# A new order for the steps between the last local-attention tile and the first softmax of the second layer

## The reference

```python
x = x + _L0_attn_ref(_layernorm(x), A, BC)        # a linear recurrence over the tokens
x = x + _L0_ffn_ref(_layernorm(x), ...)           # 2 layers of local attention (8 heads, windows of 64) with a gelu MLP
x = x + _L1_attn_ref(_layernorm(x), Wq, ...)      # full softmax attention, 8 heads of 16 columns
x = x + _L1_ffn_ref(_layernorm(x), ...)           # a shared expert and one of 32 routed experts per token
```

```python
xn = (x - mu) * rsqrt(var + LN_EPS) * gamma + beta
q = xn @ Wq + bq ; k = xn @ Wk + bk ; v = xn @ Wv + bv
scores = q @ k.T / sqrt(dk)                        # per batch and head, 512 x 512
p = softmax(scores) ; att = p @ v
out = att.reshape(S, B, D, H).sum(axis=-1)
```

## Time and profile before

| | us |
|---|---|
| median of three runs | 655.63 |
| the profiled execution, whole | 654.95 |
| its span from first to last instruction | 653.1 |
| PE busy | 594.9 (91%) |
| DVE busy | 515.4 (79%) |
| ACT busy | 364.2 (56%) |
| POOL busy | 308.8 (47%) |

### The profile page before, as it was taken

The page is one execution under the profiler, slowest core; times in us unless marked ns, Lnnn a source line. Parts: engine busy times, 40 slices in busy tenths (PEclk is TensorE's granted clock), DMA queues, the critical chain, the costliest instruction groups (busy, mean ns, idle before and its releaser), DMA issues.

```text
span 653.1 us, 14782 instructions
## 1 busy us (share of the span) xinstructions
PE 594.9 (91%) x5571; PEld 362.7 (56%) x5571; DVE 515.4 (79%) x919; ACT 364.2 (56%) x582; POOL 308.8 (47%) x254
## 2 busy tenths in 40 slices
PE   8777987999999999999999889888999989998994
PEld 7455665766766676667667566543232324454442
DVE  5887888889889798898898966877778776575883
ACT  0233453477566575674775563413765577634882
POOL 4664464556455646464665742513210010261886
PEclk8998999999999999999999999998999999998998
DMA  8413010010010101010101144151975336215441
GB/s 257 105 33 107 18 35 9 18 33 10 21 32 18 27 17 27 17 26 19 34 10 28 24 112 99 45 105 54 241 183 159 109 96 219 67 36 127 62 48 11
DMA packets 33298, 44.04 MB, mean 67 GB/s; under 512 B 9248, under 2 KB 24652, under 8 KB 32460
## 3 DMA queue, kind: packets, MB, share of 16 engines
q1 hardware_dynamic: 26172, 40.97, 23.9%
q0 software_dynamic: 3968, 2.12, 2.5%
q10 hardware_dynamic: 3088, 0.01, 0.3%
HBM read 27.54 MB, written 8.41 MB: 55 GB/s over the span
## 4 chain that ended last, share of the span: by engine, by line
PE 64%; DVE 15%; ACT 7%; issue 7%; POOL 4%; DMA 1%; POOLq 0%; DVEq 0%; SPq 0%; ACTq 0%
PE ps L1652 6%; PE ps L1683 4%; PE ps L1605 4%; PE ps L1553 3%; PE ps L1890 3%; PE ps L1661 3%; PE ps L1538 3%; PE ps L1580 3%; PE ps L1624 3%; PE ps L1788 3%; PE ps L1539 3%; PE ps L1613 3%; PE ps L1590 3%; PE ps L1544 3%; PE ps L1772 3%
## 5 line engine op out<-in xcount | busy, mean ns | idle before, releaser
L693 POOL TENSOR_TENSOR rnorm<-ssum_c,neg_half 128x16 f32<-128x16 f32 x32 | 94.7, 2960 | 102.1 <-DVE ssum_c L1099 100.7
L1328 DVE TENSOR_REDUCE mneg<-ps 128x2 f32<-128x1024 f32 x64 | 77.5, 1220 | 20.8 <-PE ps L1772 19.8
L701 POOL TENSOR_TENSOR region_r<-region_b,region_w 128x512 f32<-128x512 f32 x60 | 77.7, 1316 | 33.9 <-DVE region_b L1104 33.0
L929 ACT ACTIVATE region_r<-ps 128x1024 f32<-128x1024 f32 x64 | 63.3, 1024 | 32.3 <-PE ps L1788 32.0
L822 ACT ACTIVATE region_w<-ps 128x1024 f32<-128x1024 f32 x32 | 32.8, 1025 | 59.9 <-PE ps L1539 57.1
L658 POOL TENSOR_TENSOR var_eps<-mv,eps 128x4 f32<-128x4 f32 x20 | 11.3, 563 | 95.7 <-DVE mv L1041 95.1
L785 POOL DMA_INDIRECT out<-region_r x24 | 38.3, 1596 | 21.0 <-DVE region_r L1455 13.8
L798 ACT ACT_TABLE_LOAD x37 | 47.5, 1283 | 1.4 <-PEq L2037 0.7
L1652 PE MATMUL ps<-region_w 128*114 128x512 f32 x96 | 46.0, 603 | 1.2
L1126 DVE TENSOR_REDUCE smx<-ps 128x8 f32<-128x1024 f32 x32 | 38.9, 1217 | 9.4 <-PE ps L1580 9.4
L1605 PEld LDWEIGHTS ps<-region_b,pts 128*64 128x64 f32 x512 | 32.2, 137 | 24.5 <-issue 24.5
(11 more groups left out here) (291 smaller groups left out, 1455.0 us busy)
## 6 DMA issues: line engine op xcount, KB each, us to landing
region_w<-in_wx SPq DMA_DIRECT2D x16, 768.0 KB, 5.0
region_b<-region_w SPq DMA_DIRECT2D x56, 130.0 KB, 2.3
parts_dram<-region_b SPq DMA_DIRECT2D x6, 384.0 KB, 2.6
xs_dram<-region_w SPq DMA_DIRECT2D x1, 1548.0 KB, 7.3
region_w<-in_wqkv SPq DMA_DIRECT2D x2, 768.0 KB, 8.8
pts<-xs_dram SPq DMA_DIRECT2D x24, 64.0 KB, 2.1
region_w<-parts_dram SPq DMA_DIRECT2D x3, 384.0 KB, 6.6
region_b<-parts_dram SPq DMA_DIRECT2D x3, 384.0 KB, 7.5
```

Source lines behind the costliest of these rows:

```text
L693: g.tensor_tensor(rnorm[:, :], ssum_c[n % 2][:, :], neg_half[:, :], ALU.pow).then_inc(S["rnormed"], 1)
L701: g.tensor_tensor(dst, src, tab, ALU.mult).then_inc(S["rot_bb"], 1)
L929: act_(dst, bank(l1_bank[what, b, i], of=2), ACT.Exp).then_inc(T["ex"], 1)
L1328: d.tensor_reduce(mneg[b % 2][:, 2 * i:2 * i + 2], bank(l1_bank[what, b, i], of=2) .rearrange("p (q t) -> p q t", q=2), AX.X, ALU.max, neg ...
```

## The change

It changes the order of steps, not what any step computes; three groups of edits. The number of maxima in the drain goes from 13 to 14, LEAD from 22 to 20, and the two tables of `l1_steps()` and the hand-written drain are rewritten. The first drain maxima stand on alternating pairs of banks. Keep-busy matmuls in the drain stand ahead of maxima 12 and 13 only (before: 9 to 12).

```diff
-LEAD = 22
-DRAIN_MAX = 13
+LEAD = 20
+DRAIN_MAX = 14
...
-            early = {13: (("stat", 2), ("val", 1)), 14: (("apply", 2),), 15: (("pre", 2),), 16: (("qk", 2),),
-                     17: (("val", 2),), 18: (("split", 2),), 20: (("load", 2),)}
-            late = {1: (("stat", 3),), 3: (("apply", 3),), 6: (("pre", 3),), 8: (("qk", 3),), 9: (("split", 3),), 13: (("load", 3),), 17: (("val", 3),),
+            early = {16: (("val", 0), ("val", 1)), 17: (("stat", 2),), 18: (("apply", 2),), 19: (("pre", 2),)}
+            late = {0: (("qk", 2),), 1: (("split", 2),), 2: (("stat", 3),), 3: (("load", 2), ("apply", 3)), 4: (("val", 2),), 6: (("pre", 3),),
+                    8: (("qk", 3),), 9: (("split", 3),), 14: (("load", 3),), 18: (("val", 3),),
                     43: (("rstat", 0), ("rstat", 1)), 44: (("rapply", 0),), 45: (("rapply", 1),), 47: (("rpre", 0),), 48: (("rpre", 1),),
...
-                     ("down", 5), *l1("max"), ("wo", 30), *l1("wv")],
-                31: [("probs", 31), *l1("max", i=1), ("to_gelu", 18), *l1("stat", b=1), ("vals", 31), *l1("max", i=2),
-                     ("up", 18), ("base", 6), ("oT", 31), *l1("max", i=3), ("up", 19), ("wo", 31)]}
+                     ("down", 5), *l1("max"), *l1("max", i=1), ("wo", 30), *l1("wv")],
+                31: [("probs", 31), *l1("max", i=2), ("to_gelu", 18), ("vals", 31), *l1("stat", b=1), ("up", 18), ("base", 6), ("oT", 31),
+                     *l1("max", i=3), *l1("max", i=4), ("wo", 31)]}
...
-            yield "y_att", b
-            yield from l1("max", i=4)
+            yield from (("y_att", b), ("up", m - 5), ("shift", b))
             yield from l1("zero")
-            yield "shift", b
             yield from l1("zero", b=1)
             yield from (("ff_stats", b), ("ff_rstd", b))
             yield from l1("apply", b=1)
-            yield from (("up", m - 4), ("ff_apply", b))
             yield from l1("max", i=5)
+            yield "up", m - 4
             yield from l1("pre", b=1)
+            yield "ff_apply", b
+            yield from l1("max", i=6)
+            yield from l1("qk", b=1)
             yield "hnT", b
-            yield from l1("qk", b=1)
-            yield from l1("sums")
-            yield from l1("max", i=6)
+            yield from l1("max", i=7)
+            yield "up", m - 3
+            yield from l1("max", i=8)
+            yield from l1("max", i=9)
             yield from l1("split", b=1)
             yield "down", b - 1
-            yield from l1("max", i=7)
-            yield from (("base", b), ("up", m - 3))
-            yield from l1("val")
-            yield from l1("max", i=8)
+            yield from l1("max", i=10)
+            yield "base", b
+            yield from l1("max", i=11)
             yield "up", m - 2
             yield from l1("load", b=1)
-            yield from l1("max", i=9)
             yield from (("up", m - 1), ("to_exp", m - 1))
-            yield from l1("max", i=10)
-            yield from l1("max", i=11)
             yield from l1("max", i=12)
+            yield from l1("max", i=13)
+            yield from l1("sums")
             yield "down", b
...
-                l1_bank[what, n, i] = {"pre": 2, "val": 2, "qk": 6 if n else 0}.get(what, {0: 0, 1: 6, 2: 0, 12: 6}.get(i, 4))
+                l1_bank[what, n, i] = {"pre": 2, "val": 2, "qk": 6 if n else 0}.get(what, {0: 0, 2: 0, 4: 6, 8: 6, 10: 0, 12: 6}.get(i, 4))
...
-                if what == "l1" and n[0] == "max" and n[2] > 8:
+                if what == "l1" and n[0] == "max" and n[2] > 11:
                     keep_busy_b(2, 3)
```

## The result

The changed kernel took 660.68 us (median of 7 runs, 659.83 to 664.01), the kernel before 656.6 us beside it (median of 7, 654.35 to 658.71): ratio 1.0085, 95% interval 1.0055 to 1.0115. By the ratio, which goes by the single runs and not by the two medians, that is 5.6 us slower (3.6 to 7.5) where 2.2 us were forecast; the two medians alone lie 4.1 us apart. Measured again later with 12 runs beside 29 of before: 1.0098 (1.0068 to 1.0128).

A forecast was written before the change was run, and what follows sets the result against it. No engine is full throughout, so the order of steps sets the time. Terms -2.9 - 3.6 + 4.0 + 0.9 + 3.8 = +2.2 us on 655.63 gave 657.8 us, range 652.0 to 661.2.

The forecast's parts named there:

- The drain term: Drain: block 7's last sum starts at 433.45 instead of 436.31, -2.9 us (bounds -3.5 and -1.5).
- the last shift: End of the loop: batch 3's shift stands behind both statistics groups; all later PE work queues behind the waiting probs 48.
- The clock term: Lead: half clock behind PE's longer wait before batch 2's transposes costs between 0 and 1.7 us, taken as 0.8.
- the lead: From block 7's last sum to probs 0: 13.8 us instead of 17.4, -3.6 us (bounds -4.5 and -2.0).
- third rival: Slower: PE at half clock from the lead's transpose to the end of qk 2, +5.1 us in all, 660.7; chance 0.22.
- the loop's start: probs 0 to probs 8: 17.2 us instead of 13.2 with batch 2's steps added, +4.0 us (bounds +2.0 and +5.0).
- the shifts and the last round: Loop: shifts of batches 1 and 2 lose their slack, +0.9 us; later last maximum and batch 3's shift, +3.8 us.
- The rival that the shifts cost nothing: Loop: the waiting probs never stands, 0 instead of 0.9 and about 2.2 instead of 3.8; -0.3 us, 655.3; chance 0.20.
- VectorE's hindrance: Drain: maxima 12 and 13 and two weight sums hold block 7's last sum from 433.0 to 433.45; without them -3.5 us.
- The rival that batch 2's steps vanish in the loop: Faster: at the loop's start only about 1 us of PE work shows, shifts free; -4.2 us, 651.4; chance 0.13.
- the first sign of a right forecast: Drain: the last sum of block 7 on VectorE stands near 433.4.
- a listed sign of a wrong one: Drain: up 21 starts later than 419, where 417.7 was forecast.

The follow-up runs named there:

- e7: Changed kernel with 17 more keep-busy matmuls ahead of batch 2's transposes in the lead; 660.77 us, ratio 1.0102 to the kernel before.
- e3: Kernel before with the changed kernel's drain (14 maxima), LEAD 22 and the old loop tables kept; 657.58 us, ratio 1.0045.
- e5: e3 with block 7's gelu products in a second buffer; 653.3 us, ratio 0.9977 to the kernel before.
- e14: e9 with e7's keep-busy matmuls and 12 more in the drain; 658.06 us, ratio 1.0036 to the kernel before.
- e17: The kernel before, unaltered, profiled once more; lead 15.68 us, last stage 83.32 us, no timed run given.
- e6: Changed kernel with batch 2's qk, split, load and val moved from the loop back into the lead; 664.27 us, ratio 1.0163 to the kernel before.
- e9: Changed kernel with up 21 put back behind down 6 and maximum 10 on banks 4 and 5; 659.53 us, ratio 1.0113 to the kernel before.
- e1: Changed kernel with block 7's gelu products in a second buffer; 660.99 us, ratio 1.012 to the kernel before.

## Why the prediction was wrong

**The drain term (-2.9) is the step that failed.** It said of `up 21`: "it no longer stands behind `down 6`. From there PE goes on." It does on PE, and the start was nearly right: 22.70 us behind block 5's last sum, against 20.69 in the forecast. About half of these 2.0 us is the projections at half clock (1.99 and 1.86 us against 1.10 and 1.02); in e7, which ran them at full clock, `up 21` starts after 21.64 us. But its product still depended on `down 6` through the one `act` buffer, and moving it ahead of `down 6` put that wait at the head of VectorE's queue, with maxima 8 and 9, which PE needed, behind it. VectorE idled 5.52 us ahead of the product, and the drain came out at +3.1 instead of -2.9. The forecast names what is queued behind a waiting instruction at the last shift, and not here. The three sides of the proof: the wait of 5.52 us moves with the drain (e3), with a second buffer the product waits only for its gelu and the drain falls to 37.88 us (e5), which is about what the forecast had (39.99 - 2.9 = 37.1), and with order and clock mended the change costs 2.4 us (e14).

**The clock term was mis-sized.** 0.8 us was taken for the half clock behind the lead's wait; e7 shows 2.4 us in the first profile of after and 1.7 in the second. Within the lead 0.8 was right (1.0 and 0.8); what the forecast costed at nothing is the 1.4 and 0.9 us that the half clock takes in the start of the loop. This is the third rival's mechanism, at 1.6 and 0.9 above my 0.8 where it said 2.9. The Trainium skill (TensorE: Matmul & The Clock Gate, Part 1) says that the lower rate is the default and that activity releases it; the rows of e7, where added matmuls kept the clock up, agree. e17 shows that the half clock need not come behind a wait of 3.23 us. That the rival's total (660.7) is the measured one is luck: the larger part of the miss is in the drain.

**Right:** the lead (-3.7 against -3.6, and with the wait that was named), the loop's start but for the clock (18.73 - 14.69 = +4.0 in e7 against +4.0), the shifts and the last round (+4.0 against +4.7; the wait of each first `probs` is in the rows). The rival that the shifts cost nothing is refuted in size for batch 3 and nearly true for batches 1 and 2 (0.20 and 0.57 us of waiting, 0.20 and 0.19 in the second profile). Two sums of the forecast are a little off and change nothing: the lead's terms on VectorE reach 442.9 and not 442.7, and without VectorE's hindrance the drain's term is -3.3 and not -3.5. The rival that batch 2's steps vanish in the loop is refuted (e6, e7).

**Not foreseen by any rival:** -2.7 us in the last stage. It hides part of the miss: up to batch 3's last sum the change costs 8.5 us in the profiles, so that the total came as near to the forecast as it did is luck too.

Of the named signs, the last sum of block 7 (433.4 forecast) came at 442.31, which fails the first sign of a right forecast; `up 21` at 420.59 (419.7 on the axis of before) meets a listed sign of a wrong one. PE's idle time of over 4 us ahead of the transposes with the lower clock behind it, and the waits of the first `probs` for the shift's rows, came as listed.

## What to carry to other kernels

Before a step is moved ahead of another, look up every semaphore that its consumers wait for, not only its own: a step whose result goes into a single buffer is tied to the last reader of that buffer, and if it is issued earlier, its wait only moves to the head of a queue. Where PE waits some 2 to 4 us, as here, count the matmuls behind the wait at both clock levels; idle matmuls on a free bank in that wait shortened the two stages here by 1.7 to 2.4 us, though the timed runs of e7 alone do not show it clear of their spread. And when one comparison gives no difference for an edit that moves a stage by 2 us, put both kernels on the same chip with more runs before believing either.

## What the hardware showed that I had not expected

- The same instructions behind the same wait of 3.23 us run at full clock in one execution and at half in another (keep-busy matmuls 0.81 or 1.49 us for three; lead 15.68 or 17.37 and 18.34 us).
- Behind waits of 1.00 and 1.58 us (after) or of 2.26 us (e9) in the drain the next two `up`s took 6.25 and 5.29 us instead of 3.60; in three profiles (the first of after, e1, e3) batch 1's projections ran at half clock behind waits of 0.94, 0.42 and 0.25 us, and in others, e7 and e9 for two, at full clock behind nearly the same.
- A DMA scatter some 60 us behind the last step that was moved lands 1 us sooner or later (SyncE waits 3.5 to 3.7 or 4.5 to 4.8 us), with unchanged instructions around it: late in the eight profiles with 5571 or more matmuls, among them all four of the old order, and early in the eleven with 5567 or fewer, among them both of after.
